# One block for the whole program, and a rebuilt opening of each stage, in a convolution and spline kernel

## The chip, the cores and the metric

The kernel runs on one core of a Trainium2 chip. The metric is the device time of one execution in microseconds (us). A core has TensorE (PE, matmuls; PEld is its weight load), VectorE (DVE), ScalarE (ACT), GpSimd (POOL) and SyncE (SP), which here only starts transfers. The engines run their own instruction streams in order and meet through semaphores. DMA queues move data between the two memories.

## What is computed

The reference, cut to what matters. The image is 32 x 64 x 56 x 56 in float32.

```python
w1b, w2b = sign(w1), sign(w2)
out = relu(batchnorm(conv3x3(x, w1b), gamma1, beta1))     # statistics over all 32 images
out = batchnorm(conv3x3(out, w2b), gamma2, beta2)
x = relu(out + x)

x_aff = clip(x * a + b, -1.5, 1.5)
u = (x_aff + 1) * 0.5 * (K - 1)                           # K = 32 knots, R = 8 splines
i = floor(u); t = u - i
spline = sum over k of alpha_table[clip(i - 1 + k)] * cubic_basis_k(t)
y = id_gain * x + einsum('bchwr,cr->bchw', spline, mix) + bias
```

## The kernel before

Two images form a pair, which fills the 128 partitions (64 channels each); there are 16 pairs. Three stages follow one another, since each batch normalisation needs the statistics of all images: convolution 1 (pairs 0 to 15 in the counting of the code), convolution 2 (pairs 16 to 31), and the spline (32 chunks, each half a pair, 128 x 1568 values).

**A pair in a convolution.** SP loads it into `xin[b]` (two buffers, b = pair mod 2). The float32 values are split into two float16 parts: ACT writes the high part (value / 64), DVE the low part (what is left). In convolution 2 the input is the stored result of convolution 1, so ACT first applies normalisation and relu in place (L387), to the image and to the two halo rows that the two halves of an image need from each other (`halo`); then it writes the halo's high part (L391) and the image's (L393), and DVE the low parts (L474, L490). PE runs 9 taps x 2 parts x 4 quadrants of 64 x 64 into each of four PSUM tiles (k = 0 to 3) of 7 rows each per half image. The split buffers have a zero border of one element (58 x 58), so that each matmul covers 7 x 56 = 392 columns. ACT copies the four tiles out in two parts (`evacuate`, L414: part 0 after k = 1, part 1 after k = 3), DVE takes statistics from the copy (L524), SP stores it (L277).

**The order in convolution 2.** `rounds` writes a first and a last round out and puts the six between into a hardware loop; a round has two pairs. On ACT a pair g + 1 is normalised and split while PE works on pair g, then the two parts of g are copied out. On SP the order is: load g + 2, store g, load g + 3, store g + 1. A load waits for DVE to have read its buffer, a store for both parts of `evacuate`. So the load of pair g + 3 stands behind the store of pair g.

**Between the stages.** `norm` forms scale and bias from the last statistics (a chain of small DVE operations with one matmul and one square root). Then `first_bands` splits pair 16 in two pieces, so that PE can begin with the first. After convolution 2 `spline_constants` forms more constants, the block of the convolutions ends and that of the spline begins, with a barrier of all engines between.

**The spline.** For chunk c: `total` (sum with x), `position` (ACT), `fixed` (DVE clamps), `cells` (ACT, the cell number in bf16), `spread` (16 DMAs of 98 KB that bring the cell numbers of four groups of channels side by side into `cell4`), then masks `cell4` >= threshold (two `middle` on DVE, two `edge` on ACT; for chunk 0 all four on DVE, L1046), and PE sums five tables (near, far, square, linear, value) as mask x coefficient matmuls, which DVE combines with powers of the offset. The tables alternate between two PSUM halves, `tab[0]` and `tab[1]`.

## Time and profile before

| what | us |
|---|---|
| median of 3 runs (lowest to highest) | 1164.68 (1160.93 to 1167.83) |
| the profiled execution | 1162.34 |
| its span | 1160.5 |
| convolution 1, first matmul to last | 9.7 to 208.4 |
| convolution 2, first matmul to last | 217.6 to 419.7 |
| spline, first matmul to last | 445.3 to 1151.5 |

PE is busy for 94% of the span, DVE 82%, ACT 78%. The page's slices show PE below nine tenths only at the start, around 210 us and around 430 us. The granted TensorE clock is 0.98 in the mean, and 1.00 outside those places. The outputs of the profile that are used: the chain of waits, the groups of instructions, the timeline, the landing times of the DMAs and busy time by stretches.

### The profile page before, as it was taken

How to read it: one execution, taken by the hardware profiler on the slowest of the kernel's cores; microseconds unless marked ns; L12 is line 12 of the kernel's file. 1: busy time of each engine (PE TensorE's matmuls, PEld its weight loads, DVE VectorE, ACT ScalarE, POOL GpSimd, SP SyncE). 2: the span in 40 equal slices, each digit the busy share in tenths (PEclk: the TensorE clock that was granted, in tenths of full speed). 3: DMA queues.
4: the chain of work that ended last, by engine and by line, in shares of the span. 5: the costliest groups of instructions: out<-in, count | busy, mean ns of one | idle time of the engine just before them, and what ended most of it. 6: DMA issues, size and time to landing. Idle time of an engine off the chain costs nothing.

```text
span 1160.5 us, 51486 instructions
## 1 busy us (share of the span) xinstructions
PE 1093.0 (94%) x23818; PEld 751.4 (65%) x23818; DVE 954.2 (82%) x891; ACT 909.4 (78%) x451; POOL 138.6 (12%) x219
## 2 busy tenths in 40 slices
PE   6999999699999946999999999999999999999996
PEld 4678888578888833665666656665656766665664
DVE  5855656585665777999999999999999999999987
ACT  4435443678788627999999999999999999999971
POOL 7000000058000000011010110110110101101100
PEclk9999999899999977999999999999999999999998
DMA  6766765667767766899999989989999999999652
GB/s 229 260 257 256 278 241 224 229 236 279 278 256 281 289 249 169 189 218 228 220 218 230 218 214 236 220 216 237 215 220 222 213 230 212 225 217 219 147 134 85
DMA packets 58225, 260.95 MB, mean 225 GB/s; under 512 B 16336, under 2 KB 16336, under 8 KB 50000
## 3 DMA queue, kind: packets, MB, share of 16 engines
q1 hardware_dynamic: 48880, 209.20, 55.7%
q0 software_dynamic: 8640, 48.17, 22.7%
q8 instruction: 141, 2.31, 0.9%
q10 hardware_dynamic: 544, 1.10, 0.3%
q14 instruction: 20, 0.16, 0.0%
HBM read 104.29 MB, written 77.07 MB: 156 GB/s over the span
## 4 chain that ended last, share of the span: by engine, by line
PE 60%; DVE 1%; issue 1%; ACTq 0%; ACT 0%; DVEq 0%
PE tab L1161 52%; PE tab L1170 8%; ACTq L949 0%; DVE lin L1120 0%; DVE poly L1116 0%; DVE zbuf L1024 0%; DVE lin L1012 0%; DVE far_sq L1085 0%; DVE poly L1091 0%; DVE middle_mask L1046 0%; ACT zbuf L933 0%; ACT cell L941 0%; DVE lin L1018 0%; DVE offset L1032 0%; DVEq L1084 0%
## 5 line engine op out<-in xcount | busy, mean ns | idle before, releaser
L1161 PE MATMUL tab<-edge_mask,diag 128*32 128x392 bf16 x10240 | 446.8, 329 | 5.9 <-issue 5.9
L1161 PEld LDWEIGHTS tab<-edge_mask,diag 128*32 128x32 f16 x10240 | 277.1, 97 | 168.9 <-issue 28.4
L981 ACT ACTIVATE edge_mask<-cell,thr 128x6272 bf16<-128x6272 bf16 x62 | 338.6, 5508 | 0.5 <-DMA cell<-cell 0.5
L414 ACT ACTIVATE yout<-acc 128x1568 f32<-128x1568 f32 x64 | 94.2, 1472 | 163.0 <-PE acc L715 140.8
L1161 PE MATMUL tab<-middle_mask,diag 128*32 128x392 bf16 x4096 | 186.9, 332 | 26.8 <-DVE middle_mask L1046 22.9
L715 PE MATMUL acc<-band_split,w 64*64 64x392 f16 x4608 | 198.6, 330 | 9.9 <-ACT band_split L372 6.5
L715 PE MATMUL acc<-split,w 64*64 64x392 f16 x4608 | 196.5, 330 | 11.2 <-DVE w L467 9.7
L715 PEld LDWEIGHTS acc<-band_split,w 64*64 64x64 f16 x4608 | 164.3, 107 | 44.0 <-issue 14.8
L715 PEld LDWEIGHTS acc<-split,w 64*64 64x64 f16 x4608 | 154.5, 107 | 52.4 <-issue 11.8
L1161 PEld LDWEIGHTS tab<-middle_mask,diag 128*32 128x32 f16 x4096 | 110.3, 98 | 91.5 <-DVE middle_mask L1046 23.0
L524 DVE BATCH_NORM_STATS2 stats<-yout 128x392 f32 (+1 forms) x240 | 118.0, 555 | 60.8 <-ACT yout L414 60.0
L1039 DVE TENSOR_SCALAR middle_mask<-cell,thr 128x6272 bf16<-128x6272 bf16 x62 | 114.4, 1846 | 0.0
L910 POOL DMA_DIRECT2D lin<-far x32 | 50.2, 1569 | 524.4 <-DVE far L1070 524.4
L1170 PE MATMUL tab<-poly,ident 128*128 128x392 f32 x256 | 92.8, 505 | 0.0
L490 DVE SCALAR_TENSOR_TENSOR band_split<-band_split,xin 128x1568 f16<-128x1568 f16 x30 | 52.5, 1792 | 35.8 <-ACT band_split L393 35.8
L1063 DVE SCALAR_TENSOR_TENSOR far<-tab,first,far 128x1568 f32<-128x1568 f32 x31 | 57.4, 1851 | 27.1 <-PE tab L1161 27.1
L1170 PEld LDWEIGHTS tab<-poly,ident 128*128 128x128 f32 x256 | 46.0, 189 | 37.1 <-issue 10.4
L956 ACT ACTIVATE poly<-offset 128x1568 f32<-128x1568 int32 x32 | 48.4, 1511 | 27.2 <-DVE offset L1032 27.2
L501 DVE SCALAR_TENSOR_TENSOR split<-split,xin 128x3136 f16<-128x3136 f16 (+4 forms) x19 | 55.1, 2911 | 10.5 <-ACT split L404 10.3
L1077 DVE SCALAR_TENSOR_TENSOR poly<-tab,first,dist_sq 128x1568 f32<-128x1568 f32 x31 | 57.4, 1850 | 6.5 <-PE tab L1170 6.5
L933 ACT ACTIVATE zbuf<-lin,cst 128x1568 f32<-128x1568 f32 x32 | 53.9, 1684 | 11.1 <-issue 6.0
L1070 DVE SCALAR_TENSOR_TENSOR far<-far,cst,far_sq 128x1568 f32<-128x1568 f32 x32 | 59.3, 1852 | 1.1
(133 smaller groups left out, 956.2 us busy)
## 6 DMA issues: line engine op xcount, KB each, us to landing
y_scratch<-yout SPq DMA_DIRECT2D x32, 1568.0 KB, 6.2
cell<-cell SPq DMA_DIRECT2D x504, 98.0 KB, 5.0
xin<-y_scratch SPq DMA_DIRECT2D x16, 1568.0 KB, 9.1
lin<-far POOLq DMA_DIRECT2D x32, 784.0 KB, 9.5
out<-lin SPq DMA_DIRECT2D x31, 784.0 KB, 5.6
xin<-in_x SPq DMA_DIRECT2D x15, 1568.0 KB, 9.3
lin<-y_scratch SPq DMA_DIRECT2D x30, 784.0 KB, 9.5
lin<-in_x POOLq DMA_DIRECT2D x28, 784.0 KB, 7.7
```

The lines of the kernel that those rows point to most:

```text
L414: act.activation(yout[b][:, :].rearrange("p (r k x) -> p k r x", r=2, k=TILES)[:, 2 * part:2 * part + 2], acc[:, 4 * part:4 * part + 4, 0: ...
L501: dve.scalar_tensor_tensor(out=inner(split[b][1], first, end), in0=inner(split[b][0], first, end), scalar=-SPLIT, in1=rows(xin[b], first, ...
L524: dve.bn_stats(stats[:, bass.ds(COUNTS * (g - base) + t, 1), :], yout[b][:, own]).then_inc(counted, 1)
L715: mm = pe.matmul(acc[h * C:(h + 1) * C, 2 * k + r, 0:TILE], weights[part][own, tap * C:(tap + 1) * C], image[own, first:first + ROWS, dx:d ...
L933: act.activation(place[c % 2][:, :], lin_of(c)[:, :], ACT.Identity, bias=cc(U_B), scale=cc(U_S)).then_inc(place_ready, 1)
L981: act.activation(mask_of(c, q)[:, :, :], cell4[c % 2][:, :, :], ACT.Sign, bias=thr[:, q:q + 1]).then_inc(sign_mask_ready, 1)
L1039: dve.tensor_scalar(mask_of(c, q)[:, :, :], cell4[c % 2][:, :, :], thr[:, q:q + 1], None, ALU.is_ge).then_inc(mask_ready, 1)
L1063: dve.scalar_tensor_tensor(out=quarters(far[c % 2]), in0=summed(c, T_FAR), scalar=base(c, T_FAR), in1=quarters(far[c % 2]), op0=ALU.add, o ...
L1070: dve.scalar_tensor_tensor(out=far[c % 2][:, :], in0=far[c % 2][:, :], scalar=cc(AMP), in1=far_sq[:, :], op0=ALU.mult, op1=ALU.mult).then_ ...
L1077: dve.scalar_tensor_tensor(out=quarters(poly[c % 2]), in0=summed(c, T_SQ), scalar=base(c, T_SQ), in1=quarters(dist_sq), op0=ALU.add, op1=A ...
L1161: mm = pe.matmul(tab[(c + t) % 2][j * GROUP:(j + 1) * GROUP, sub, 0:SUB], keep["diag"][part][:, j % 2, t, q, :], mask_of(c, q)[:, j, sub * ...
L1170: return pe.matmul(tab[(c + T_SQ) % 2][:, sub, 0:SUB], keep["ident"][:, :], poly[c % 2][:, sub * SUB:(sub + 1) * SUB], start=False, stop=True)
```

## The change

**One block.** `build` opens one block, which both functions use; the barrier between convolution 2 and the spline goes. Where the spline's buffers lie on those of the convolutions, `conv_buffers_free` waits for the last stores of `y2`. Of `spline_constants` only the position's bias stays ahead of the spline (`position_bias`); the rest moves into `value_constants`, which DVE runs after the first masks.

**Convolutions.** The split buffers have no zero border. The centre tap comes first and writes the whole tile; the other taps leave out the columns and rows that fall outside (55 of 56 columns for six of nine taps; 6 of 7 rows for three taps at the image's top and for three at its bottom). The memsets of borders (8 on DVE, 24 on POOL) go.

**Convolution 2.** The halo's normalisation and high part move from ACT to DVE (four more small operations a pair). ACT normalises pair g + 2 inside `evacuate` of pair g, between its two parts. The opening pair's high part is made straight from the raw values, with scale and bias divided by 64, in three pieces (8, 7 and 13 rows of each half); its in-place normalisation follows for the low part.

**The spline's opening.** Chunk 0 is summed, positioned and clamped in halves. Its cells are spread by PE: for each half, 32 matmuls of 392 columns with columns of the identity put them into `tab[0]` and `tab[1]`, and ACT (three) and DVE (one) copy them into `cell4`. The masks of chunk 0 are made in halves, and PE's near table of chunk 0 goes half by half. ACT and DVE have an order of their own up to chunk 1.

```diff
@@ hi_parts and evacuate, ACT
+                if conv == 1 and isinstance(g, int) and g < PAIRS + 2:
+                    act.wait_ge(loaded[b], 16 * (half_rounds - 1 + b) + 48)
...
+                    normalise(b, i)
...
                     act.activation(yout[b][:, :].rearrange("p (r k x) -> p k r x", r=2, k=TILES)[:, 2 * part:2 * part + 2],
...
+                    if part == 0 and normalise_next:
+                        normalise(b, i + 1)
@@ ACT
+            def normalise(b, i):
+
+                act.wait_ge(loaded[b], 16 * (half_rounds - 1 + b) + 48 * (i - half_rounds + 1))
+                act.activation(xin[b][:, :], xin[b][:, :], ACT.Relu, bias=cst[:, BN1_B:BN1_B + 1],
+                               scale=cst[:, BN1_S:BN1_S + 1]).then_inc(normed, 1)
@@ taps, PE
+                for tap, part in TAP_PARTS:
...
+                    dy, dx = tap // 3 - 1, tap % 3 - 1
+                    cols = slice(max(0, -dx), W - max(0, dx))
+                    from_cols = slice(max(0, dx), W - max(0, -dx))
@@ spline, PE
+            def spread_cells(h, s):
+
+                pe.wait_ge(cell_ready if h else cell_half, 1)
+                if h:
+                    pe.wait_ge(taken_by_dve if s else taken_by_act, 1)
...
+                            mm = pe.matmul(tab[s][g * GROUP:(g + 1) * GROUP, 2 * (j % 2) + u, 0:SUB],
+                                           ones[:, 2 * GROUP * j + 1:2 * GROUP * (j + 1):2],
+                                           cell[0][:, (2 * h + u) * SUB:(2 * h + u + 1) * SUB], start=True, stop=True)
@@ spline, ACT
+            for h in range(2):
+                position_half(h)
+            conv_buffers_free(act)
+            for h in range(2):
+                cells_half(h)
+            take_spread(0, 0)
+            position(1)
+            take_spread(1, 0)
+            take_spread(1, 1)
```

The order of the instructions moves at three places. First, ACT in the loop of convolution 2. Before, one half of the loop body (`yout` is the copy out of PSUM, `xin` the pair in place, `band_split` its high part):

```order
L387 ACTIVATE xin1<-xin1,cst 128x3136 [waits x_loaded1]
L387 ACTIVATE halo1<-halo1,cst 128x112
L389 ISA
L391 ACTIVATE band_split10<-halo1 64x2x56 [waits normed]
L391 ACTIVATE band_split10<-halo1 64x2x56
L393 ACTIVATE band_split10<-xin1 128x2x28x56
L70 REGISTER_ALU
L70 ISA [waits y_stored0]
L413 REGISTER_ALU [waits counted]
L414 ACTIVATE yout0<-acc 128x2x2x392 [waits tile_done]
L413 REGISTER_ALU
L414 ACTIVATE yout0<-acc 128x2x2x392 [waits tile_done]
```

After, the same half of the body:

```order
L388 ACTIVATE band_split10<-xin1 128x2x1568 [waits normed]
L72 REGISTER_ALU
L72 ISA [waits y_stored0]
L408 REGISTER_ALU [waits counted]
L409 ACTIVATE yout0<-acc 128x2x2x392 [waits tile_done]
L369 ISA
L370 ACTIVATE xin0<-xin0,cst 128x3136 [waits x_loaded0]
L408 REGISTER_ALU
L409 ACTIVATE yout0<-acc 128x2x2x392 [waits tile_done]
```

The wait for a load (`x_loaded`) stood ahead of both copies and was for the next pair; now it stands between the two copies and is for the pair after that. SP's order is as it was.

Second, DVE where the spline begins. Before:

```order
L91 UNCONDITIONAL_BRANCH [waits spline_constants_ready]
L1005 UNCONDITIONAL_BRANCH [waits barrier_Pool_Activation_PE_DVE_SP_release]
L1012 SCALAR_TENSOR_TENSOR lin<-zbuf,cst,lin 128x1568 [waits x_loaded_for_sum0,y_loaded0]
L1012 SCALAR_TENSOR_TENSOR lin<-zbuf,cst,lin 128x1568 [waits x_loaded_for_sum1,y_loaded1]
L1024 TENSOR_SCALAR zbuf<-zbuf,cst 128x1568 [waits place_ready]
L1032 TENSOR_SCALAR offset<-zbuf 128x1568 [waits fixed_point_ready]
L1018 TENSOR_SCALAR lin<-lin,cst,par_sb 128x1568 [waits place_ready]
L1012 SCALAR_TENSOR_TENSOR lin<-lin,cst 128x1568 [waits x_loaded_for_sum2,y_loaded2]
```

After:

```order
L1095 SCALAR_TENSOR_TENSOR lin<-zbuf,cst,lin 128x784 [waits x_loaded_for_sum0,y_loaded0] x2
L1101 TENSOR_SCALAR zbuf<-zbuf,cst 128x784 [waits first_half_place_ready]
L1101 TENSOR_SCALAR zbuf<-zbuf,cst 128x784 [waits place_ready]
L1087 SCALAR_TENSOR_TENSOR lin<-zbuf,cst,lin 128x1568 [waits x_loaded_for_sum1,y_loaded1]
L1108 CAST cell<-tab 128x2x784 [waits cells_spread_by_pe,y_stored1,y_stored0]
L1155 TENSOR_SCALAR middle_mask<-cell,above 128x4x784 [waits spread_taken_by_dve,spread_taken_by_act]
L1155 TENSOR_SCALAR middle_mask<-cell,above 128x4x784
L1131 TENSOR_SCALAR zbuf<-zbuf,cst 128x1568 [waits place_ready]
L1155 TENSOR_SCALAR edge_mask<-cell,above 128x4x784 [waits spread_taken_by_dve,spread_taken_by_act]
L1155 TENSOR_SCALAR edge_mask<-cell,above 128x4x784
L1139 TENSOR_SCALAR offset<-zbuf 128x1568 [waits fixed_point_ready]
```

The barrier is gone, the masks move ahead of the later sums, offsets and linear parts, and a copy out of PSUM is new. Third, PE at the same place has these rows ahead of what was its first spline row (`tab<-middle_mask`):

```order
L1308 MATMUL tab<-cell,ident 32x392 [waits first_half_cell_ready,pool_chain]
L1308 MATMUL tab<-cell,ident 32x392 x15
L1308 MATMUL tab<-cell,ident 32x392 [waits first_half_cell_ready]
L1308 MATMUL tab<-cell,ident 32x392 x15
L1308 MATMUL tab<-cell,ident 32x392 [waits spread_taken_by_act,cell_ready]
L1308 MATMUL tab<-cell,ident 32x392 x15
L1308 MATMUL tab<-cell,ident 32x392 [waits spread_taken_by_dve,cell_ready]
L1308 MATMUL tab<-cell,ident 32x392 x15
L1287 MATMUL tab<-middle_mask,diag 32x392 [waits first_half_mask_ready,spread_taken_by_act]
```

Sixty-four matmuls come in, and the first table waits for a mask of a half chunk and for ACT's second copy.

## Rows read from the trace of the kernel before

**Rows 1.** The page: busy time and share by engine, and the chain.
```profile
PE 1093.0 (94%) x23818; PEld 751.4 (65%) x23818; DVE 954.2 (82%) x891; ACT 909.4 (78%) x451; POOL 138.6 (12%) x219
PE 60%; DVE 1%; issue 1%; ACTq 0%; ACT 0%; DVEq 0%
```

**Rows 2.** Timeline of ACT in convolution 2: start, duration, line, what, idle before.
```profile
319.44 1.48 ACT L414 ACTIVATE yout<-acc 128x1568 f32<-128x1568 f32 x1 [2.51 <-PE acc L715]
320.81 2.99 ACT L387 ACTIVATE xin<-xin,cst 128x3136 f32<-128x3136 f32 x1
...
324.86 2.82 ACT L393 ACTIVATE band_split<-xin 128x3136 f16<-128x3136 f32 x1
...
331.70 1.48 ACT L414 ACTIVATE yout<-acc 128x1568 f32<-128x1568 f32 x1 [2.67 <-PE acc L715]
```

**Rows 3.** Timeline of SP's queue in the same stretch.
```profile
320.94 0.36 SPq L277 DMA_DIRECT2D y_scratch<-yout  x1
321.99 0.34 SPq L273 DMA_DIRECT2D xin<-y_scratch  x1
322.43 2.60 SPq L273 DMA_DIRECT2D halo<-y_scratch  x2
333.21 0.37 SPq L277 DMA_DIRECT2D y_scratch<-yout  x1
334.00 0.33 SPq L273 DMA_DIRECT2D xin<-y_scratch  x1
```

**Rows 4.** The tile xin, 260 to 400 us: its loads, issue to landing.
```profile
DMA to landing us min/median/max: 8.8/8.9/9.2
```

**Rows 5.** The tile halo, 260 to 400 us: its loads, issue to landing.
```profile
DMA to landing us min/median/max: 7.7/8.1/9.0
```

**Rows 6.** The page, DMA issues: stores of the convolutions, median us to landing.
```profile
y_scratch<-yout SPq DMA_DIRECT2D x32, 1568.0 KB, 6.2
```

**Rows 7.** Page and groups by line: busy us, mean ns, idle before.
```profile
L715 PE MATMUL acc<-split,w 64*64 64x392 f16 x4608 | 196.5, 330 | 11.2 <-DVE w L467 9.7
L490 DVE SCALAR_TENSOR_TENSOR band_split<-band_split,xin 128x1568 f16<-128x1568 f16 x30 | 52.5, 1792 | 35.8 <-ACT band_split L393 35.8
L941 ACT ACTIVATE cell<-zbuf,cst 128x1568 bf16<-128x1568 uint16 x32 | 50.9, 1589 | 5.1 <-DVE zbuf L1024 5.1
L1018 DVE TENSOR_SCALAR lin<-lin,cst,par_sb 128x1568 f32<-128x1568 f32 x32 | 34.9, 1091 | 0.0
```

**Rows 8.** Timeline, opening and end of convolution 2.
```profile
212.77 0.22 DVE L660 SCALAR_TENSOR_TENSOR cst<-mean,cst,par_sb 128x1 f32<-128x1 f32 x1
...
217.57 24.22 PE L715 MATMUL acc<-band_split,w 64*64 64x392 f16 x511 [6.46 <-ACT band_split L372]
...
221.68 3.00 ACT L387 ACTIVATE xin<-xin,cst 128x3136 f32<-128x3136 f32 x1 [1.27 <-DMA halo<-y_scratch]
...
233.69 0.35 SPq L277 DMA_DIRECT2D y_scratch<-yout  x1
...
392.56 1.48 ACT L414 ACTIVATE yout<-acc 128x1568 f32<-128x1568 f32 x1 [2.51 <-PE acc L715]
...
420.77 1.48 ACT L414 ACTIVATE yout<-acc 128x1568 f32<-128x1568 f32 x1 [3.91 <-DVE stats L510]
```

**Rows 9.** Timeline, opening of the spline.
```profile
424.28 0.22 DVE L621 SCALAR_TENSOR_TENSOR cst<-cst 128x1 f32<-128x1 f32 x1
...
426.31 3.61 DVE L1012 SCALAR_TENSOR_TENSOR lin<-zbuf,cst,lin 128x1568 f32<-128x1568 f32 x2 [0.98 <-PEq L91]
...
443.38 3.61 DVE L1046 TENSOR_SCALAR middle_mask<-cell,above 128x6272 bf16<-128x6272 bf16 x2
...
445.28 5.42 PE L1161 MATMUL tab<-middle_mask,diag 128*32 128x392 bf16 x64 [22.92 <-DVE middle_mask L1046]
...
491.00 2.83 PE L1161 MATMUL tab<-middle_mask,diag 128*32 128x392 bf16 x64
```

**Rows 10.** Stretches: PE, PEld, DVE, ACT, POOL busy (instructions), granted clock, DMA share, GB/s.
```profile
445.00:447.00 2.00, 1.72 (x24) 0.88 (x28) 2.00 (x3) 2.00 (x2) 0.00 (x0) 0.50 0.68 158
```

More of the change, by code:

```diff
@@ L18 @@
 PX = H * W
-HP, WP = H + 2, W + 2
 TAPS = 9
+CENTRE = 4
+TAP_PARTS = ((CENTRE, 0), *((tap, part) for tap in range(TAPS) if tap != CENTRE for part in range(2)), (CENTRE, 1))
 ROWS = 7
@@ L209, in halo_row @@
             row = HB - 1 if band == 0 else 0
-            return bands(t)[own, :, row, 1:W + 1]
+            return bands(t)[own, :, row, :]
         def halo_of(t, band):
@@ L375, in hi_parts @@
-            def hi_parts(g, b, i, conv):
+                act.wait_ge(bn_ready, 1)
+                for n, (first, end) in enumerate(BAND_PIECES):
+                    act.activation(split_bands(b, 0, first, end), x_bands(b, first, end), ACT.Relu,
+                                   bias=cst[:, BN1_B_HI:BN1_B_HI + 1],
+                                   scale=cst[:, BN1_S_HI:BN1_S_HI + 1]).then_inc(band_hi, 1)
+                    if n == 0:
+                        continue
+                    for m in ((0, 1) if n == 1 else (n,)):
+                        act.wait_ge(band_hi, m + 1)
+                        act.wait_ge(bn_plain_ready, 1)
+                        start, stop = BAND_PIECES[m]
+                        act.activation(x_bands(b, start, stop), x_bands(b, start, stop), ACT.Relu,
+                                       bias=cst[:, BN1_B:BN1_B + 1],
+                                       scale=cst[:, BN1_S:BN1_S + 1]).then_inc(normed, 1)
@@ L478, in lo_parts @@
                     if split_up(g, conv):
-                        for early, (first, end) in zip((True, False), BAND_PIECES):
-                            dve.wait_ge(band_early_hi if early else hi_done, 1 if early else late(g))
+                        for n, (first, end) in enumerate(BAND_PIECES):
+                            dve.wait_ge(band_hi, n + 1)
+                            dve.wait_ge(normed, n + 1)
                             for r in range(2):
@@ L855, in lin_of, with copies, half, spread_half @@
             return lin[c % LIN]
+        def copies(c):
+            return 256 * (c // 2 + c % 2)
+        def half(t, h):
+            return t[:, h * 2 * SUB:(h + 1) * 2 * SUB]
+        def spread_half(h, s):
+            return (cell4[0][:, 2 * s:2 * s + 2, h * 2 * SUB:(h + 1) * 2 * SUB].rearrange("p j (u x) -> p j u x", u=2),
+                    tab[s][:, :, 0:SUB].rearrange("p (j u) x -> p j u x", u=2))
+        def conv_buffers_free(eng):
+            for b in range(2):
+                eng.wait_ge(keep["y_stored"][b], 16 * PAIRS)
         @block.sync
@@ L1121, in closing_quarters @@
                                              in1=lin_of(c)[:, own], op0=ALU.mult, op1=ALU.add).then_inc(whole, 1)
-            total(0)
+            for h in range(2):
+                total_half(h)
+            for h in range(2):
+                fixed_half_chunk(h)
             total(1)
-            for c in range(2):
-                fixed(c)
-                offsets(c)
-                linear(c)
-                if c == 0:
-                    total(2)
-            first_masks()
-            total(3)
-            for c in range(CHUNKS):
-                if c > 0:
-                    value(c - 1)
+            conv_buffers_free(dve)
+            take_spread(0, 1)
+            first_masks(0, MIDDLE_QUADS)
+            fixed(1)
+            first_masks(0, EDGE_QUADS)
+            offsets(0)
+            first_masks(1, QUAD_ORDER)
+            value_constants()
+            total(2)
+            near_cube(0)
+            fixed(2)
+            total(3)
+            far_cube(0)
+            linear(0)
+            far_part(0)
+            middle(1, MIDDLE_QUADS[0])
+            square(0)
+            offsets(1)
+            slope(0)
+            middle(1, MIDDLE_QUADS[1])
+            add_slope(0)
+            linear(1)
+            linear(2)
+            for c in range(1, CHUNKS):
+                value(c - 1)
                 if c + 2 < CHUNKS:
@@ L1200, in table @@
                 mm.then_inc(table_ready, 1)
+            pe.wait_ge(*keep["diag_ready"])
+            for h in range(2):
+                for s in range(2):
+                    spread_cells(h, s)
+            first_table()
+            pe.wait_ge(taken_by_act, 3)
             for c in range(CHUNKS):
                 for t in range(TABLES):
-                    table(c, t)
+                    if (c, t) != (0, T_NEAR):
+                        table(c, t)
 def build(nc, x, w1, w2, par_dram, mix_t, alpha_t, out):
```

303 lines of the change are left out of this document (178 added, 125 removed).

## The prediction

> **What bounds the kernel now.** I read the page's busy shares first, then the chain, then the timeline where PE pauses. PE is busy for 94% of the span and holds 60% of the chain [rows 1]; the chain runs back only as far as the spline's start. In the spline PE goes from chunk to chunk with gaps of 0.3 to 1.5 us that no engine ends; that stage is not touched past chunk 1. In the convolutions PE is the bound too: ACT sits idle for 2.5 to 2.7 us before a copy until PE has finished [rows 2]. The places where PE itself waits are the openings: 6.5 us before its first matmul of convolution 2 (217.57, while the bias was ready at 212.99) [rows 8], and 22.9 us before the spline's first (445.28, while the position's bias was ready at 424.50) [rows 9]. The change aims at these and at the matmuls' columns. What I look at hardest is a thing that costs nothing today: when a load lands. Let E(g) be the end of the second copy of pair g, and let an arrow mean "releases".
>
> **Convolution 1, fewer columns.** A pair takes 288 matmuls; four quadrants run side by side. 196.5 us for 4608 is 170.6 ns for a group of four [rows 7], near 163.3 ns, which is 392 columns at 2.4 GHz, so columns are what PE pays. Six of nine taps lose 7 of 392 columns: 16 pairs x 4 tiles x 6 taps x 2 parts = 768 groups, each 2.9 ns shorter: 2.2 us. The rows cut at top and bottom touch only two quadrants of a group at a time; if half of it counted it would be worth another 2.2 us (16 x 2 tiles x 3 taps x 2 parts = 192 groups, 23.3 ns each, halved). I take nothing for it, since each group still has two full quadrants. Bounds: 0 (if matmuls of short rows cost their old time) to 4.5. The Trainium skill ("TensorE: Matmul & The Clock Gate", Measured speedup vs the span model) says that matmuls start and end in strict order; by it the cut rows give nothing and the term stays 2.2, and no row here shows it. The memsets of borders hide: DVE waited 5.2 us for weights after them, and PE waits for DVE's weights [rows 7]. They cost nothing and bring nothing.
>
> **Opening of convolution 2.** Now the first piece's high part comes straight after the bias: 896 values on ACT, 1.0 us instead of 4.5, so PE starts near 214.5, 3.1 us earlier. But pair 17 follows the old clock: its load lands at 221.68 as before [rows 8], then 2.9 (normalise) + 2.8 (high) + 3.5 (low, two of 1.79) [rows 2, 7] = 231 us, where pair 17 began near 232 before. ACT then copies pair 16, normalises pair 18 and copies again: 227.4 + 1.4 + 2.9 + 1.5 = 233.2, against 233.7 for the store before [rows 8]. DVE still has its 6 us of table steps ahead of pair 18. So the 3.1 us are gone by pair 18, and I count 0 for the opening (bounds -3.1 to +0.5).
>
> **The loop of convolution 2: a wait that is new.** The order on the three queues now closes a ring: E(g) -> SP stores g, then loads g + 3 -> it lands -> ACT normalises g + 3 -> ACT's second copy of g + 1, which is E(g + 1). Queued behind the waiting normalise are that copy, SP's store of g + 1 and so its load of g + 4, and the high part of g + 3. Before, the normalise stood ahead of both copies for a pair one later, so nothing that SP waits for stood behind it; ACT came to it 320.81 - 321.99 + 12.2 = 11.0 us after the load's issue, and it was there. Ring, link by link:
> - E to the load's issue: 321.99 - 320.92 = 1.07, and 334.00 - 333.18 = 0.82 [rows 2, 3]; mean 0.95.
> - Issue to landing: the image 8.9 [rows 4]; the halo's second DMA is issued 1.7 later [rows 3] and takes 7.7 to 8.1 [rows 5], so 9.4 to 9.8. I take 9.5. Bounds 8.9 and 10.2, the wait that pair 17's load gave (issued 211.47, landed 221.68).
> - Normalise 2.99, of which 0.1 overlaps, as 320.81 against 320.92 shows: 2.9 [rows 2].
> - The second copy 1.48 [rows 2].
> Sum 14.8 us for a pair, against (392.56 - 319.44) / 6 = 12.19 now [rows 2, 8]. The landing doesn't shrink when pairs come slower, since the store that is in front of it in the same 16 engines (6.2 us to landing [rows 6]) is always issued just before it. From E(17), which stays near 247.4, to E(29) are 12 rounds of the ring: 247.5 + 12 x 14.83 = 425.5, against 394.0: +31.5. Pairs 30 and 31 have no normalise inside. Before, they took PE 27.1 us from 392.56 to 419.7, so pair 31 started about 12.1 after E(29); now it starts when its high and low parts are there, 2.8 + 3.5 + 0.6 for DVE's halo rows = 6.9 after. That gives back 5.2. Net +26.2 us (bounds by the landing: -0.6 x 12 = -7 and +0.7 x 12 = +8). PE's fewer columns and the halo's move hide behind the ring; if the ring were not there, the columns would be worth 2 us here as well.
>
> **The spline's opening.** Times from the ready bias (before: 424.50). The old path: barrier and constants 1.8, sum, position, clamp, cells, 8 issues on ACT, masks; PE at +20.8, chunk 2's first matmul at +66.5 [rows 9]. The new: sums in halves 1.9, positions to 2.9; then ACT waits for the last store of y2, issued after 420.77 + 1.48 and landing 6.2 later [rows 6, 8], which is +4.0. Cells 4.9 and 5.8 (half of 1.59 each and a little [rows 7]). PE spreads: 16 matmuls at 84.7 ns (5.42 / 64, at a granted clock of 0.50, 1.2 GHz [rows 9, 10]) = 1.4: 6.3 and 7.7. ACT copies (1.5) to 7.8, positions chunk 1 to 9.4, copies again to 10.9, and PE's first table can begin: 9.9 us sooner. It doesn't stay so. DVE is a single file from here: its copy to 9.6, eight half masks of 0.9 (two full ones take 3.61 [rows 9]), a clamp and offsets: 18.7; constants, two sums, near, far, far part, mask, square, slope at 1.8 each and clamp, linear, offsets at 1.0 [rows 7, 9]: the slope of chunk 0 at 36.9, which frees PSUM for chunk 1's near table. Then a mask, the addition, two linears, value, clamp, linear, near, finish, far, far part, mask, square, offsets, slope: 59.9, and chunk 2's first matmul at 60.5. Gain 6.0. Later DVE's chunk (about 21) is shorter than PE's 21.5, so that 6.0 stays. Bounds: 9.9 if DVE keeps up, 2 if copies out of PSUM and chunk 1's 16 DMAs come some 4 us later; no row shows a bf16 copy of this form.
>
> **The sum.** -2.2 + 26.2 - 6.0 = +18.0 on the profiled execution's 1162.34 (span 1160.5 and 1.8 around it): 1180.3. That execution lies 2.3 below the median of three, so I put it at 1181.5.
>
> **Rivals.**
> - *The loads land in time* (faster). The ring binds only if E to landing takes over 12.19 - 2.9 - 1.48 = 7.8 us; I read 10.4. The store, of the same size, lands in 6.2 [rows 6]; were the load to land so too, the ring would be 11.5 and PE would stay the bound. Then -2.2 - 2.0 - 6.0: 1152. Against it: 8.9 is the median of loads issued at just this point [rows 4]. The Trainium skill ("DMA: Bandwidth & Descriptors", Measured) gives 6.15 us for 1 MB alone and 425 GB/s for large ones, so an estimate from that page for 1.6 MB alone is under 7 us, which is this rival; the row, with the store ahead, says 8.9. Chance 0.13.
> - *The ring is half closed*: landing and overhead come to about 9, period 13.4, conv 2 +10: 1165. Chance 0.06, within 0.5% or just above.
> - *PE's clock falls too* (slower still). In the ring PE waits twice a pair, about 2.7 us together. The clock was 0.50 after pauses of 6.5 and 22.9 us [rows 8 to 10], 1.00 through the spline's gaps of up to 1.5. At 1.2 GHz a pair takes 24.2 us and PE enters the ring: (6.9 + 24.2 + 1.5) / 2 = 16.3 a pair, +1.5 x 12 = +18: 1199. Chance 0.07.
> - *The opening brings nothing*: PE's first table is early but chunk 2 is not: 1187, inside the forecast's own range.
>
> **How the numbers follow.** Forecast 0.74, its own range 1170 to 1193: the landing's bounds -7 and +8, conv 1 +-2.2, opening -4 and +4, not all at once. Left out are the fast rival and part of the slow one; the range goes from 1169 to 1196. A measurement can tell 0.5%, 5.8 us. Faster 0.13, same 0.05, slower 0.82.
>
> **What would show it.** In the trace after: ACT's idle time before the in-place normalise of convolution 2, ended by the DMA of xin or halo, some 5 to 6 us a pair (today 1.3 in all); pairs 14.8 us apart there and 12.0 in convolution 1; SP's stores 14.8 apart; PE waiting for ACT's copies and DVE's low parts. PE's first spline matmul (the spread) near +4.9 from the bias, the first table near +10.9, chunk 2 near +60.5. Wrong would be: pairs of convolution 2 at 12.1 us, or no wait on a load.

## The result and the profile after

| | us |
|---|---|
| before, median of 4 runs (lowest to highest) | 1164.74 (1160.93 to 1167.83) |
| after, median of 4 runs | 1189.2 (1185.92 to 1191.67) |
| ratio, 95% interval | 1.021 (1.0169 to 1.0251) |
| after, the profiled execution and its span | 1191.67, 1189.9 |

The changed kernel is slower by 24.5 us. The forecast was 1181.5 in a range of 1169 to 1196: right in sign and in mechanism, short by 7.7 us at the median. Against the same execution as before, 1162.34, the profiled one is 29.3 us longer; the terms below are worked out for that.

The page of after, busy time by engine, the chain by engine and by line, the two groups that changed most, and the loads of convolution 2 (last column: us to landing):

```profile
PE 1096.3 (92%) x23882; PEld 744.1 (63%) x23882; DVE 970.3 (82%) x959; ACT 897.8 (75%) x410; POOL 135.5 (11%) x195
...
PE 76%; DMA 10%; issue 6%; DVE 3%; ACT 3%; SPq 2%; ACTq 0%; DVEq 0%
...
L730 PE MATMUL acc<-band_split,w 64*64 64x385 f16 (+3 forms) x4608 | 202.7, 333 | 38.8 <-ACT yout L409 17.5
...
L370 ACT ACTIVATE xin<-xin,cst 128x3136 f32<-128x3136 f32 x15 | 45.0, 3002 | 87.7 <-DMA halo<-y_scratch 87.7
...
xin<-y_scratch SPq DMA_DIRECT2D x16, 1568.0 KB, 8.9
```

Three things differ from [rows 1]. DMA has a tenth of the chain, where it had no share. PE waited 38.8 us in convolution 2, where it had waited 9.9. And ACT's in-place normalise (L370) waited 87.7 us for loads to land, where the same instruction waited 1.3 before. The landing itself is the 8.9 us of [rows 4].

One turn of the ring, ACT in the middle of convolution 2 (columns as in [rows 2]):

```profile
334.92 3.00 ACT L370 ACTIVATE xin<-xin,cst 128x3136 f32<-128x3136 f32 x1 [6.50 <-DMA halo<-y_scratch]
337.83 1.46 ACT L409 ACTIVATE yout<-acc 128x1568 f32<-128x1568 f32 x1
339.19 2.81 ACT L388 ACTIVATE band_split<-xin 128x3136 f16<-128x3136 f32 x1
...
349.94 3.00 ACT L370 ACTIVATE xin<-xin,cst 128x3136 f32<-128x3136 f32 x1 [6.59 <-DMA halo<-y_scratch]
```

SP's queue in the same stretch:

```profile
324.38 0.37 SPq L279 DMA_DIRECT2D y_scratch<-yout  x1
325.17 0.33 SPq L275 DMA_DIRECT2D xin<-y_scratch  x1
325.61 2.61 SPq L275 DMA_DIRECT2D halo<-y_scratch  x2
339.31 0.36 SPq L279 DMA_DIRECT2D y_scratch<-yout  x1
340.36 0.34 SPq L275 DMA_DIRECT2D xin<-y_scratch  x1
```

Read it as a circle. SP issues the store at 324.38 and the load at 325.17. ACT's normalise is released at 334.92, 9.75 after the load's issue. The second copy follows at 337.83 and ends at 339.29; at 339.31 SP issues the next store. The turn takes 14.93 us. PE is not a link of it: it waits 1.3 us twice a pair, once for ACT's copies and once for DVE's low parts.

```profile
331.94 6.17 PE L730 MATMUL acc<-band_split,w 64*64 64x392 f16 x144 [1.28 <-DVE band_split L498]
339.43 5.87 PE L730 MATMUL acc<-band_split,w 64*64 64x392 f16 x138 [1.31 <-ACT yout L409]
```

The spline's opening, all engines (DVE's 453.12 row makes the position's bias, ready at 453.34):

```profile
451.12 0.35 SPq L279 DMA_DIRECT2D y_scratch<-yout  x1
...
453.12 0.22 DVE L632 SCALAR_TENSOR_TENSOR cst<-cst 128x1 f32<-128x1 f32 x1
...
460.53 1.79 ACT L1005 ACTIVATE cell<-zbuf,cst 128x784 bf16<-128x784 uint16 x2 [3.83 <-DMA y_scratch<-yout]
461.62 2.81 PE L1308 MATMUL tab<-cell,ident 128*32 128x392 bf16 x32 [10.42 <-ACT cell L1005]
...
467.87 1.58 PE L1287 MATMUL tab<-middle_mask,diag 128*32 128x392 bf16 x32 [0.30 <-ACT cell L1012]
...
517.51 2.66 PE L1287 MATMUL tab<-middle_mask,diag 128*32 128x392 bf16 x60
```

ACT could not write the cells before the last store of `y2` had landed; the wait ended 9.4 us after that store's issue. Chunk 2's first matmul came 64.2 us after the bias.

The whole difference by stage, each from the instants of this trace and of [rows 8, 9] (stores of pairs 17 and 29: 247.39 and 394.06 before, 246.27 and 429.16 after):

| stretch | before | after | difference | forecast |
|---|---|---|---|---|
| start to the ready bias of convolution 1 | 212.99 | 208.85 | -4.1 | -2.2 |
| to the store of pair 17 | 34.4 | 37.4 | +3.0 | 0 |
| 12 rounds, to the store of pair 29 | 146.7 | 182.9 | +36.2 | +31.5 |
| to the position's bias | 30.4 | 24.2 | -6.3 | -5.2 |
| to chunk 2's first matmul | 66.5 | 64.2 | -2.3 | -6.0 |
| to the end of the span | 669.5 | 672.4 | +2.9 | 0 |

I take the last row as scatter between executions and not as a part of the change: in the eleven kernels of the experiments below whose code is the same from there on (all but x2) it was 666.1 to 673.4 us, in one execution each.

### The profile page after: what moved, and what is told of

Same layout as the page of the kernel before. It is cut to its first block, busy times and chain, and to the rows that moved or that the text cites. A ratio compares the mean times of both kernels' runs of the same rounds, so it can differ in the third digit from the quotient of the medians.

```text
span 1189.9 us, 51640 instructions
## 1 busy us (share of the span) xinstructions
PE 1096.3 (92%) x23882; PEld 744.1 (63%) x23882; DVE 970.3 (82%) x959; ACT 897.8 (75%) x410; POOL 135.5 (11%) x195
## 3 DMA queue, kind: packets, MB, share of 16 engines
q8 instruction: 142, 2.33, 0.9%
## 4 chain that ended last, share of the span: by engine, by line
PE 76%; DMA 10%; issue 6%; DVE 3%; ACT 3%; SPq 2%; ACTq 0%; DVEq 0%
PE tab L1287 48%; PE acc L730 19%; DMA halo<-y_scratch 9%; PE tab L1296 7%; ACT yout L409 2%; SPq L275 2%; DMA y_scratch<-yout 1%; ACT xin L370 1%; DMA w_raw<-in_w 1%; SPq L279 0%; DVE edge_mask L1155 0%; DVE far_sq L1195 0%; DVE poly L1201 0%; DVE middle_mask L1155 0%; DVE lin L1125 0%
## 5 line engine op out<-in xcount | busy, mean ns | idle before, releaser
L730 PE MATMUL acc<-band_split,w 64*64 64x385 f16 (+3 forms) x4608 | 202.7, 333 | 38.8 <-ACT yout L409 17.5
L730 PEld LDWEIGHTS acc<-band_split,w 64*64 64x64 f16 x4608 | 167.1, 110 | 74.1 <-issue 44.4
L730 PE MATMUL acc<-split,w 64*64 64x385 f16 (+3 forms) x4608 | 191.5, 326 | 12.1 <-DVE w L457 10.3
L730 PEld LDWEIGHTS acc<-split,w 64*64 64x64 f16 x4608 | 145.2, 108 | 57.7 <-issue 12.7
L370 ACT ACTIVATE xin<-xin,cst 128x3136 f32<-128x3136 f32 x15 | 45.0, 3002 | 87.7 <-DMA halo<-y_scratch 87.7
L1173 DVE SCALAR_TENSOR_TENSOR far<-tab,first,far 128x1568 f32<-128x1568 f32 x31 | 57.4, 1851 | 29.5 <-PE tab L1287 29.3
L509 DVE SCALAR_TENSOR_TENSOR split<-split,xin 128x3136 f16<-128x3136 f16 (+4 forms) x19 | 55.0, 2909 | 10.5 <-ACT split L399 10.2
L1166 DVE SCALAR_TENSOR_TENSOR poly<-tab,first,poly 128x1568 f32<-128x1568 f32 x31 | 57.3, 1847 | 5.2 <-PE tab L1287 5.2
```

The costliest lines, as they stand in the source:

```text
L370: act.activation(xin[b][:, :], xin[b][:, :], ACT.Relu, bias=cst[:, BN1_B:BN1_B + 1], scale=cst[:, BN1_S:BN1_S + 1]).then_inc(normed, 1)
L730: mm = pe.matmul(to[:, top:end, cols], weights[part][own, tap * C:(tap + 1) * C], image[own, first + dy + top:first + dy + end, from_cols] ...
L1166: dve.scalar_tensor_tensor(out=quarters(poly[c % 2]), in0=summed(c, T_NEAR), scalar=base(c, T_NEAR), in1=quarters(poly[c % 2]), op0=ALU.ad ...
L1173: dve.scalar_tensor_tensor(out=quarters(far[c % 2]), in0=summed(c, T_FAR), scalar=base(c, T_FAR), in1=quarters(far[c % 2]), op0=ALU.add, o ...
```

## Experiments

Times are medians; "before" was run beside them, 1163.62, 1163.63 and 1162.77 in the three groups (x1 to x4; x5 to x9; x10 to x13).

### The ring: undone, and made alone

ACT's normalise behind both copies, nothing else changed:

```diff
-                    if part == 0 and normalise_next:
-                        normalise(b, i + 1)
+                if normalise_next:
+                    normalise(b, i + 1)
```

> The changed kernel with one thing undone: ACT's in-place normalise of pair g + 2 stands behind both copies of pair g, not between them. Theory (a ring of store, load, normalise and second copy sets the pace of convolution 2, 15.2 us a pair in the changed kernel's trace from 246.27 to 429.16 in 12 pairs): the stores of convolution 2 come 11.8 to 12.0 us apart, ACT's wait for the load before the normalise falls from 87.7 us in all to under 10, and the time falls by about 12 x 3.3 = 39, less the 6 us that the end of the convolution gave back, and some 3 more because the last store lands faster: about 1153. Rival 1 (PE's matmuls of short rows, or DVE's halo operations, slow convolution 2): it stays within 5 us of the changed kernel's 1189. Rival 2 (the loads are slower by themselves, wherever they are waited for): ACT still waits some 6 us a pair and the time is above 1175.

Measured: 1150.65 us (1150.28 to 1151.13), ratio to before 0.9891 (0.9864 to 0.9919). The group of the normalise and two of ACT's rows, in the trace of this kernel:

```profile
L370 ACT ACTIVATE xin<-xin,cst 128x3136 f32<-128x3136 f32 x15 | 44.9, 2993 | 2.3 <-DMA halo<-y_scratch 2.3
```
```profile
327.84 1.48 ACT L409 ACTIVATE yout<-acc 128x1568 f32<-128x1568 f32 x1 [3.24 <-PE acc L730]
329.21 2.99 ACT L370 ACTIVATE xin<-xin,cst 128x3136 f32<-128x3136 f32 x1
```

The wait falls from 87.7 to 2.3 us, although the loads still take 8.9 us to land; stores are 11.82 us apart and PE is the bound again. One instruction's place is worth 38.5 us, and the change is then worth 13 us.

The opposite: the kernel before, with only the in-place normalise (and the halo's) put between the two copies.

```diff
...
+                for t in (xin[b], halo[b]):
+                    act.activation(t[:, :], t[:, :], ACT.Relu, bias=cst[:, BN1_B:BN1_B + 1],
...
+                    if part == 0 and normalise_next:
+                        normalise(b, i + 1)
```

> The kernel before with one part of the change alone: the in-place normalise (image and halo rows) of pair g + 2 is moved between the two copies of pair g; halo on ACT, padded buffers, two blocks and the old openings all stay. Theory: the ring closes here too. A link is 0.95 + 9.7 to the landing + 2.9 + 0.5 (halo) + 1.5 = 15.5 us against 12.2; 12 links +39, less 5 to 6 at the end: about 1198. Rival (the ring needs other parts of the change, for instance the halo's move to DVE): 1165, as before.

Measured: 1199.01 us, ratio 1.0301 (1.027 to 1.0332), 35.4 us more than before. ACT's rows in its trace show the same wait, and the stores stand 15.3 apart (299.78 to 437.68 for nine rounds):

```profile
325.71 3.00 ACT L379 ACTIVATE xin<-xin,cst 128x3136 f32<-128x3136 f32 x1 [5.90 <-DMA halo<-y_scratch]
...
340.97 3.00 ACT L379 ACTIVATE xin<-xin,cst 128x3136 f32<-128x3136 f32 x1 [5.80 <-DMA halo<-y_scratch]
```

So the place of the normalise is enough to make the loss, without any other part of the change.

### The link that can be shortened: the landing

SP issues the load of pair g + 3 ahead of the store of pair g, instead of behind it; ACT's order stays as changed.

```diff
-                    if not is_last(n):
-                        following = load(g + 2, b, conv)
...
+                    if conv == 1:
...
+                        if not is_last(n) and not (n == 2 * half_rounds - 2 and b == 1):
+                            follow(g + 1, 1 - b)
```

> The changed kernel with ACT's order kept (normalise between the copies), but SP issues the load of pair g + 3 ahead of the store of pair g, as soon as DVE has left its buffer. The ring is cut at another link. Theory: the same gain as when the normalise moves, about 1153 (1148 to 1160); stores 11.8 to 12.2 us apart; ACT waits for the load less than 1 us a pair. Rival 1 (what costs is the place of the normalise on ACT, which holds up the copy whatever SP does): stays above 1175. Rival 2 (the loads and stores are bound by bandwidth, so that order can't matter): 1175 or more.

Measured: 1148.93 us, ratio 0.9874 (0.9846 to 0.9903). The tile `xin` from 260 to 400 us, issue to landing, and SP's queue:

```profile
DMA to landing us min/median/max: 6.0/6.1/6.2
```
```profile
318.40 0.36 SPq L287 DMA_DIRECT2D y_scratch<-yout  x1
325.73 0.34 SPq L273 DMA_DIRECT2D xin<-y_scratch  x1
...
330.22 0.37 SPq L287 DMA_DIRECT2D y_scratch<-yout  x1
```

The ring is cut open here: the load no longer stands behind the store that ACT's second copy releases, so it is issued 4.5 us ahead of the store, and it lands in 6.1 instead of 8.9. Two kernels thus undo the loss at different links, which a cause outside the ring would not allow.

A smaller dose: convolution 2 stores only the first half of each pair, and the spline reads that half twice.

```diff
-                    sp.dma_start(place, yout[b][:, :]).then_inc(stored[b], 16)
+                    if conv == 0:
+                        sp.dma_start(place, yout[b][:, :]).then_inc(stored[b], 16)
+                    else:
+                        sp.dma_start(place[:, 0:CHUNK], yout[b][:, 0:CHUNK]).then_inc(stored[b], 16)
```

> The changed kernel; in convolution 2 only the first half of each pair's result is stored, and the spline reads that half twice, so half of the second convolution's result is left out. The order of everything is kept. Theory (the load's landing in the ring is long because the store of the same size is in front of it): half of 1.6 MB at the 400 to 430 GB/s of the trace's stretches is 1.9 us less per link: stores 13.2 to 13.5 us apart, 12 x 1.9 = 23 less, plus up to 4 at the end: 1162 to 1168. Rival (the landing is latency, or the halo's many small rows, and not the store): under 5 us less, 1184 or more.

Measured: 1162.69 us, ratio 0.999 (0.997 to 1.001). Its `xin` from 260 to 400 us, and the normalise:

```profile
DMA to landing us min/median/max: 6.8/7.0/7.2
```
```profile
L373 ACT ACTIVATE xin<-xin,cst 128x3136 f32<-128x3136 f32 x15 | 45.0, 3003 | 61.5 <-DMA halo<-y_scratch 61.5
```

With the store halved the load lands 1.9 us earlier and the stores are 13.17 us apart in the mean (302.10 to 407.43, eight rounds) instead of 15.0: the period is 1.8 us shorter, nearly what the landing is. It still exceeds PE's 11.82, so a ring is left, and 61.5 us of waiting.

### Convolution 1: what the cut rows are worth

A pair of convolution 1 took 11.82 us against 12.11, which is 0.29 less. The columns explain 48 groups x 2.9 ns = 0.14. The prediction took the cut rows at nothing, because each group of four quadrants keeps two full ones. ACT's copies out of PSUM show PE's pace; two pairs' worth, of before:

```profile
75.25 1.48 ACT L414 ACTIVATE yout<-acc 128x1568 f32<-128x1568 f32 x1 [4.58 <-PE acc L715]
...
87.36 1.48 ACT L414 ACTIVATE yout<-acc 128x1568 f32<-128x1568 f32 x1 [4.58 <-PE acc L715]
```

and of after:

```profile
74.28 1.48 ACT L409 ACTIVATE yout<-acc 128x1568 f32<-128x1568 f32 x1 [4.50 <-PE acc L730]
...
86.10 1.48 ACT L409 ACTIVATE yout<-acc 128x1568 f32<-128x1568 f32 x1 [4.50 <-PE acc L730]
```

My first theory was that time goes by the mean over the four quadrants, since half of 6 groups x 2 ends x 23.3 ns is just 0.14. To test it, two of the four quadrants were shortened in all taps but the centre:

```diff
+                            if conv == 0 and h == 0 and tap != CENTRE:
+                                end = 5
```

> Leaves out a part of convolution 1: on the two quadrants of the upper image halves (h = 0) all taps but the centre write only rows up to the fifth of seven. The other two quadrants of each group of four keep their size. Base: the kernel with ACT's normalise behind both copies (pairs 11.82 us apart in convolution 1). It asks what a group of four quadrants costs when two of them are short. Theory, the mean over the quadrants: 4 tiles x 8 taps x 2 parts = 64 groups a pair, each loses about 110 columns in half of its quadrants = 23 ns, 1.47 us: pairs 10.35 us apart, convolution 1 ends about 23 us earlier, total about 1127. Rival, the longest quadrant sets it (order of start and end kept): pairs stay at 11.82, total 1150. DVE has 7.5 us of work a pair there and ACT 5.8, so they don't bind.

```profile
75.07 1.48 ACT L409 ACTIVATE yout<-acc 128x1568 f32<-128x1568 f32 x1 [4.36 <-PE acc L732]
...
86.89 1.48 ACT L409 ACTIVATE yout<-acc 128x1568 f32<-128x1568 f32 x1 [4.36 <-PE acc L732]
```

Still 11.82: the mean law is refuted, and so is my reading of the 0.29. What is left are two theories: the rows bring nothing and something else brings 0.14, or a quadrant's own sum counts. The cuts at the top fall to the upper half's quadrants (h = 0), those at the bottom to the lower's (h = 1), so that each loses 6 groups x 23.3 ns = 0.14 over a pair. Three variants of convolution 1 tell them apart; in all of them a tap whose row is not cut reads a row inside the image.

```diff
@@ whole rows
+                                top = 0
+                                end = ROWS
@@ top only
+                                top = int(dy < 0 and h == 0 and k == 0)
+                                end = ROWS
@@ both on the upper half
+                                top = int(dy < 0 and h == 0 and k == 0)
+                                end = ROWS - int(dy > 0 and h == 0 and k == TILES - 1)
```

> Changes a part of convolution 1: no row is cut at the image's top and bottom (the taps there read a row inside the image instead of none), the columns stay cut. Base: ACT's normalise behind both copies, pairs 11.82 us apart. Theory A, a quadrant runs at the pace of its own columns and may fall behind the others by part of a matmul, so that the largest sum over a pair sets the time: 6 groups x 23.3 ns = 0.14 more, pairs 11.96 apart. Theory B, the cut rows bring nothing at all (0.14 of the 0.29 came from something else, like the order of the taps): 11.82.

```profile
74.38 1.48 ACT L409 ACTIVATE yout<-acc 128x1568 f32<-128x1568 f32 x1 [4.50 <-PE acc L738]
...
86.34 1.48 ACT L409 ACTIVATE yout<-acc 128x1568 f32<-128x1568 f32 x1 [4.50 <-PE acc L738]
```

> Changes a part of convolution 1: rows are cut at the top alone, which is on the quadrants of the upper half (h = 0); the three taps at the bottom read a row inside the image. Theory A, largest sum of a quadrant: the lower half's quadrants have all their rows, so pairs 11.96 apart. Theory C, six groups whose upper quadrants are short count in full wherever they stand, and those at the bottom count nothing: 11.82.

```profile
76.36 1.48 ACT L409 ACTIVATE yout<-acc 128x1568 f32<-128x1568 f32 x1 [4.50 <-PE acc L738]
...
88.33 1.48 ACT L409 ACTIVATE yout<-acc 128x1568 f32<-128x1568 f32 x1 [4.50 <-PE acc L738]
```

> Changes a part of convolution 1: as many rows are cut as in the changed kernel, but both at the top and at the bottom on the quadrants of the upper half (h = 0). Theory A, largest sum of a quadrant: 11.96 a pair, though the mean over the quadrants is as in the changed kernel. Theory M, mean over the quadrants: 11.82. Theory C, upper quadrants count in full: 11.68.

```profile
75.46 1.48 ACT L409 ACTIVATE yout<-acc 128x1568 f32<-128x1568 f32 x1 [4.50 <-PE acc L738]
...
87.42 1.48 ACT L409 ACTIVATE yout<-acc 128x1568 f32<-128x1568 f32 x1 [4.50 <-PE acc L738]
```

All three take 11.96 or 11.97 us. Rows cut on the upper half alone bring nothing, even when as many are cut as in the changed kernel; cut on both halves, at different places of the pair, they count in full. The mean over the quadrants fails in the kernels with a short half and with both cuts on one half, the largest quadrant of each group in the changed kernel (it gives 11.96, measured 11.82). One rule fits all six: the quadrant with the largest sum over the pair sets the time, and one may fall behind its neighbours by part of a matmul and catch up later:

| cut in convolution 1 | largest sum of a quadrant, against whole | a pair, us |
|---|---|---|
| none (before) | | 12.11 |
| columns | -0.14 | 11.96 |
| columns, rows at the top | -0.14 | 11.97 |
| columns, rows at both ends, on one half | -0.14 | 11.96 |
| columns, rows at both ends, each on its half (after) | -0.28 | 11.82 |
| as after, and one half much shorter | -0.28 | 11.82 |

A rival fits the six sums as well: that the lower half's quadrants alone set the time, since none of the kernels cuts the lower half alone. The two parts of a pair speak against it. In the kernel with a short half tiles 0 and 1 take 5.98 us and tiles 2 and 3 take 5.84, as the lower half's cuts (in tile 3) would have it. In the changed kernel, whose lower half is the same, it is the other way round, 5.84 and then 5.98: the time goes in tiles 0 and 1, where only the upper half is cut. A kernel with rows cut on the lower half alone was not run, and the rule of the largest sum gives the sums, but I can't derive this order from it. (The totals of these four kernels, one execution each, were 1153.9 to 1158.1 us and say nothing here: from chunk 2 of the spline on they differ by up to 3.0 us, 670.4 to 673.4, and the pairs of all of them by 0.15 us, 2.4 over convolution 1.)

### The spline's opening: spread or barrier

On the kernel with the normalise behind both copies, the cells of chunk 0 spread by 16 DMAs again:

```diff
@@ PE
-            for h in range(2):
-                for s in range(2):
-                    spread_cells(h, s)
@@ ACT, 8 of the 16; the other 8 go out on SP
+            for g in range(2, 4):
+                for j in range(4):
+                    act.dma_start(cell4[0][g * GROUP:(g + 1) * GROUP, j, :],
+                                  cell[0][j * GROUP:(j + 1) * GROUP, :]).then_inc(copied[0], 16)
```

> The kernel with ACT's normalise behind both copies, with chunk 0's cells spread by 16 DMAs (8 issues on SP, 8 on ACT) as before, not by PE; halves of chunk 0, one block and DVE's new order stay. DVE's copy out of PSUM and ACT's three go. Theory that the spread by PE brings about half of the opening's gain: first table at the bias + 15 to 17 instead of 10.4, chunk 2's near table 3 to 5 us later than 60.2: 1154 to 1156. Rival, that DVE's single file sets chunk 2's start and has the time of the spread made good by then: within 1 us of 1150.6.

and, on the same base, the two blocks with their barrier again:

```diff
@@ in both functions
-        block = keep["block"]
+        block = ctx.enter_context(nc.Block())
```

> The kernel with ACT's normalise behind both copies, with two blocks and the barrier between convolution 2 and the spline again. Asks what the one block alone brings. The barrier stood in 1.8 us of the opening before (bias at 424.50, first sum at 426.31), part of it the constants that no longer stand there. With ACT waiting for the last store of y2 anyway until bias + 4.0, I expect that the barrier's end costs 0.5 to 2 us: 1151 to 1153. If the one block were what brought the 6 us of the opening, it would be 1156.

Rows of the base (x1; bias ready at 418.83), the first table and chunk 2's near table:

```profile
429.20 1.79 PE L1287 MATMUL tab<-middle_mask,diag 128*32 128x392 bf16 x32 [0.30 <-ACT cell L1012]
...
479.06 2.83 PE L1287 MATMUL tab<-middle_mask,diag 128*32 128x392 bf16 x64
```

Of the kernel with the DMAs (bias ready at 419.21), the first table and chunk 2's:

```profile
434.40 2.80 PE L1287 MATMUL tab<-middle_mask,diag 128*32 128x392 bf16 x32 [17.33 <-DVE middle_mask L1156]
...
484.26 2.83 PE L1287 MATMUL tab<-middle_mask,diag 128*32 128x392 bf16 x64
```

| from the ready bias, us | first table | chunk 2 |
|---|---|---|
| before [rows 9] | +20.8 | +66.5 |
| forecast | +10.9 | +60.5 |
| x1, ring undone | +10.4 | +60.2 |
| x7, DMAs spread | +15.2 | +65.1 |
| x6, barrier back | +10.7 | +60.5 |
| after | +14.5 | +64.2 |

The forecast of this stage holds within 0.5 us where the last store lands in time. Of its 6.3 us the spread by PE brings 4.8 and the barrier's end 0.3, less than the 0.5 to 2 I had expected of it. The 1.2 left over I put down to the halves and DVE's new order; no run takes these out alone. Each of these differences is between two single executions. The totals don't show them (1152.65 us for x7 with 6 runs from 1151.3 to 1155.73, and 1150.64 for x6 with 7 runs from 1143.64 to 1157.81, against 1150.65; 1154 to 1156 was expected for x7), since they carry the scatter of the 670 us behind.

Why the changed kernel gets only 2.3 of the 6.3: the stretches below give DMA share and GB/s as their last two numbers, here in its last microseconds of convolution 2,

```profile
445.00:452.00 7.00, 3.87 (x88) 3.02 (x80) 4.46 (x16) 3.16 (x3) 0.00 (x0) 1.00 1.02 394
```

and in x1 at the same point:

```profile
410.00:418.00 8.00, 3.75 (x80) 2.69 (x80) 4.02 (x15) 2.91 (x3) 0.00 (x0) 1.00 0.57 240
```

The eight loads of the spline's opening go out behind the store of pair 29. In x1 that was from 389.0 to 394.5 us, 22 to 28 us ahead of the last store (416.60), and the rush was over by then; in the changed kernel it was from 429.7 to 435.1, only 16 to 21 us ahead of it (451.12), since pair 30 comes 7.8 us behind pair 29 there and not 13.3. The store of pair 30 stands between them: in x1 it landed at 416.3, just before the last store went out, in the changed kernel at 456.7, 5.6 us behind it. The last store alone, issue to landing, in x1 and in the changed kernel:

```profile
y_scratch<-yout SPq DMA_DIRECT2D x1, 1568.0 KB, 5.2
```
```profile
y_scratch<-yout SPq DMA_DIRECT2D x1, 1568.0 KB, 9.3
```

The kernels without this part of the change agree. In x2, the kernel before with the ring, the eight loads went out 16.5 to 22 us ahead of the last store (438.26 to 443.56, and 460.08), and it took 9.3 too; in the kernel before they went out 22 to 28 us ahead, and it took 5.2. So the ring is enough to make that landing late.

### Two tries at a better version

On the kernel with the load first (1148.93): pair 17's load ahead of the last store of `y1`, and DVE's table steps behind the low part of pair 18 instead of ahead of it.

> The kernel with SP's load ahead of the store (1148.93), and in the opening of convolution 2 two moves: the load of pair 17 goes ahead of the last store of y1, and DVE's steps for the tables behind the low part of pair 18. PE waits 3.2 us before pair 17 and 1.7 before pair 18, with the next low part late by about as much (DVE's steps, 7 us, stand before pair 18's). Expected: pair 17 starts at 225 to 226 instead of 228.8, the third pair without DVE's wait, convolution 2 ends 4 to 5 us earlier: 1144 to 1145. Rival: the last store of y1, now behind, comes late or the load of 17 is bound by the same transfers: same as 1149.

Measured: 1150.22 us (1147.52 to 1153.65), no gain. PE's rows at the opening:

```profile
226.50 19.82 PE L743 MATMUL acc<-band_split,w 64*64 64x392 f16 x476 [1.26 <-issue]
247.46 4.34 PE L743 MATMUL acc<-band_split,w 64*64 64x385 f16 x100 [1.13 <-issue]
254.89 13.91 PE L743 MATMUL acc<-band_split,w 64*64 64x392 f16 x288 [3.09 <-DVE band_split L511]
```

Pair 17 starts 2.3 us earlier, but the steps, about 6 us, now make the low part of a later pair late, and PE gives the gain back: the position's bias is ready at 419.29, as in x3 (419.28). So the steps were cut in two, one part of them in the last round of convolution 1:

```diff
+                    if n == half_rounds - 1:
+                        steps()
                     if is_last(n):
                         most_of_stats(conv)
```

> The kernel with SP's load ahead of the store and pair 17's load ahead of the last store of y1 (1150.22), with DVE's table steps cut in two: 3.4 us of them in the last round of convolution 1, ahead of the statistics of its last pair, the other 2.2 behind the low part of pair 18. PE waited 3.09 us for DVE's low part of pair 19 there, with all the steps in one place. Expected: that wait falls to under 1 us, bias of batch norm 2 2.5 us earlier, 1147 to 1148. Rival: the part in convolution 1 makes the last statistics late, and the gain is gone: 1150.

Measured: 1150.24 us (1146.2 to 1153.23), where 1147 to 1148 was expected. The rival is right in part: the matmul of the last statistics of convolution 1 waits for DVE 4.25 us, where it is 2.33 in x3. That spends part of what PE saves behind. The rest is left in the trace, with the position's bias at 417.59 and chunk 2's first matmul at 477.81, both 1.7 us earlier than in x3, in one execution each; it is too small for the medians to show.

```profile
209.85 0.59 PE L825 MATMUL acc<-mv,avg 128*128 128x2 f32 x2 [4.25 <-DVE mv L666]
```

Neither median beats the kernel with SP's load first (1148.93), nor does that differ measurably from the one with the normalise moved (1150.65). Either is 13 to 15 us faster than before, and 38 to 40 faster than after.

## Why the prediction was right, and where it was short

- **The ring** was the right mechanism, and it was read from the order of three queues and two durations. Its size was off by 4.7 us: 15.24 a round instead of 14.83. The steady rounds from 309.32 to 429.16 took 14.98, because the halo released ACT 9.6 to 9.75 us after the load's issue where I took 9.5; the first four took 15.8, with releases 9.5 to 11.2 after the issue. The bounds I gave, 8.9 to 10.2, cover the mean of the twelve but not these first ones. Why they are later isn't known.
- **The opening of convolution 2**, taken at 0, cost 3.0 us. PE began early as forecast, 1.7 us after the bias. But pair 17's load released ACT 11.25 us after its issue instead of 10.2, and pair 17 waited 3.7 us for DVE's low part; up to the store of pair 16 that makes 0.6. The other 2.4 lie between the stores of pairs 16 and 17, 16.1 us apart instead of 13.7. The step that failed is that the second copy of pair 17 would stay where it was: pair 19's normalise stands ahead of it, and the load behind the store of pair 16 (issue 230.53) released that only at 241.88. There the ring had closed already, one round before I let it begin.
- **The end** gave back 6.3 us instead of 5.2, by the same mechanism.
- **Convolution 1** gave 4.1 us instead of 2.2. The columns were right (12.11 to 11.96). The rows were mis-sized: taken at 0, worth another 0.14 us a pair. The Trainium skill ("TensorE: Matmul & The Clock Gate", The mechanism) says that matmuls start and end in program order. Nothing here speaks against that; what fell is my inference from it, that a group of four costs what its longest quadrant costs. 11.82 against 11.96 us a pair shows that cuts on both halves count together, in groups that each keep two full quadrants.
- **The spline's opening** gave 2.3 us instead of 6.0. The step that failed is the last store's landing, 6.2 from [rows 6]: it took 9.3, since the ring had moved the opening's loads and the store of pair 30 against it. With the ring undone the stage came out at +60.2 against +60.5. The forecast had the pieces right one by one, and missed that the first part of the change shifts the traffic that the last part depends on.
- **The rivals.** "The loads land in time" would need a landing of 6.2; it is 8.9 behind a store and 6.1 ahead of one, and its price, 1152, is what the kernels without the ring show (1148.93 and 1150.65). The estimate of under 7 us for a lone load of 1.6 MB, which was part of this rival, doesn't follow from the figures that it names: from the Trainium skill's 6.15 us for 1 MB, and 425 GB/s for the rest, the estimate is about 7.5 us ("DMA: Bandwidth & Descriptors", Measured), and no row here shows a load that is alone. "The clock falls too" came only in two pairs of the ring and cost nothing. Through the steady rounds, with two waits of 1.3 us a pair, the clock stayed at 1.00. But PE's waits of 1.99 us (pair from 278.08) and 2.72 us (from 309.44) were each followed by some 3 us at 0.50, which is 1.2 GHz:

```profile
309.44 13.69 PE L730 MATMUL acc<-band_split,w 64*64 64x392 f16 x288 [2.72 <-ACT yout L409]
```
```profile
310.00:313.00 3.00, 3.00 (x44) 2.23 (x40) 2.74 (x10) 3.00 (x2) 0.00 (x0) 0.50 0.97 401
```

These pairs took PE 13.69 us instead of twice 6.17, and the stores still stood 15.03 and 15.06 us apart, since PE had that much time to wait.

## What to carry to other kernels

Before moving a step that waits for a load, follow the queues round: which store does it hold back, and which load stands behind that store? If the circle closes on the same instruction, add its links; a load that cost nothing with a slack of under 2 us then sets the pace of the whole loop. Putting the load ahead of the store, or the waiting step behind the last copy, opens it. And a forecast by stages should ask what an earlier stage's new pace does to the transfers that the next one waits for.

## What the hardware showed that I had not expected

- With four 64 x 64 quadrants running side by side, a pair took 11.96 us where rows were cut on the upper half alone and 11.82 where they were cut on both, on one at the pair's first tile and on the other at its last. Neither the mean nor the longest of each group gives these; the largest sum of a quadrant over the pair does, though cuts on the lower half alone were not run.
- A load of 1.6 MB took 8.9 us to land behind a store of the same size, 7.0 behind half of one, and 6.1 in front of it.
- A store of 1.6 MB landed in 9.3 us where eight loads (6.4 MB) had been issued 16 to 22 us before it (after, x2), and in 5.2 where they had been issued 22 to 28 us before (before, x1). In both cases another store of 1.6 MB stood between them.
- In the kernel before with the ring alone (x2) PE's waits of 2.07 to 2.15 us, one every second pair from 299.90 on, were each followed by a slower pair (13.96 us instead of twice 6.25); the granted clock was 0.93 from 300 to 375 us. The waits of 1.29 to 1.38 us between them were not, nor was one of 2.42 us before (284.51). The stores stayed 15.3 us apart.
